# Second attention: four tiles instead of two split and stored before the stage, and all four read as it opens

## The reference, cut to what matters

```python
x = _layernorm(x + _L1_attn_ref(x, w_qkv, w_z, w_b, w_a, conv_w, dt_bias, a_log, norm_w, w_out))   # gated delta rule
x = _layernorm(x + _L1_xattn_ref(x, ctx_2048, ctx_2048, L1_xattn_gamma))                           # second attention
x = _layernorm(x + _L1_ffn_ref(x, gate_w, w_gate, w_up, w_down))                                   # experts, top 8 of 64

def _L1_xattn_ref(q, k, v, gamma):        # B=32, Dq=64, Lq=256
    qh = q.reshape(B, 8, 8, Lq)           # 8 heads of 8 rows each
    kh = k.reshape(B, 8, 8, Lk)
    vh = v.reshape(B, 8, 8, Lk)
    qk = jnp.einsum('bhdq,bhdl->bhql', qh, kh) / sqrt(8)
    sm = jax.nn.softmax(qk, axis=-1)
    return gamma * jnp.einsum('bhql,bhdl->bhdq', sm, vh).reshape(B, 64, Lq)
```

## Time and profile before

| | us |
|---|---|
| median of three runs | 3860.91 |
| the profiled execution | 3866.17 |
| its span, first to last instruction | 3864.1 |
| the second attention, barrier to its last scatters | about 2938 to 3320 |

### The profile page before, as it was taken

One profiled execution on the slowest core, in us unless ns is written; L12 is line 12 of the kernel. 1 busy time (PEld: TensorE's weight loads), 2 busy tenths in 40 slices (PEclk: granted clock), 3 DMA queues, 4 the chain that ended last, 5 costly groups with the idle time before them and its releaser, 6 DMA issues. The chain is left out here.

```text
span 3864.1 us, 101293 instructions
## 1 busy us (share of the span) xinstructions
PE 3395.9 (88%) x37544; PEld 2305.7 (60%) x37544; DVE 2397.3 (62%) x4366; ACT 1956.2 (51%) x5232; POOL 1966.2 (51%) x2830
## 2 busy tenths in 40 slices
PE   9998799886999999999999999999985878588876
PEld 6776466554666666666666666666663544344544
DVE  5554466344777777777777777777774766233433
ACT  1111255323666666666666666666652655243434
POOL 2232433243666556656555566655563455455654
PEclk9999799997999999999999999999996988699998
DMA  2000543001211111111111211111103543355545
GB/s 77 11 16 7 141 114 92 25 1 37 58 47 45 50 43 53 46 46 47 39 50 44 57 47 39 47 46 49 45 21 78 130 129 108 133 172 169 181 133 215
DMA packets 223140, 278.85 MB, mean 72 GB/s; under 512 B 58548, under 2 KB 186872, under 8 KB 216280
## 3 DMA queue, kind: packets, MB, share of 16 engines
q1 hardware_dynamic: 203340, 237.24, 21.5%
q0 software_dynamic: 18432, 34.96, 2.6%
q10 hardware_dynamic: 908, 0.27, 0.1%
HBM read 162.13 MB, written 125.83 MB: 75 GB/s over the span
## 5 line engine op out<-in xcount | busy, mean ns | idle before, releaser
L2153 PE MATMUL head_ring<-gd_xT,head_w 128*128 128x512 f32 x1024 | 522.7, 635 | 15.2 <-DMA head_w<-gd_w 10.4
L2607 POOL TENSOR_TENSOR head_V<-head_V,gd_ones 128x512 bf16<-128x512 f32 x128 | 133.0, 1040 | 476.1 <-DVE head_V L2451 476.1
L1504 POOL DMA_INDIRECT ytok<-exp_arena,exp_cur x256 | 250.6, 979 | 201.0 <-ACT exp_arena L1407 122.8
L2426 DVE SCALAR_TENSOR_TENSOR head_cb_V<-head_ring,head_taps,head_cb_V 128x504 f32<-128x504 f32 (+2 forms) x384 | 280.0, 729 | 12.9 <-ACT head_cb_V L2303 8.2
L2153 PEld LDWEIGHTS head_ring<-gd_xT,head_w 128*128 128x128 f32 x1024 | 182.8, 199 | 155.5 <-issue 132.5
L2272 PE MATMUL head_by<-head_wo,head_ogT 128*128 128x256 f32 x1024 | 258.2, 396 | 9.5 <-issue 6.1
L2162 PE MATMUL head_ring<-head_w,gd_xT 128*128 128x256 f32 x1024 | 256.0, 393 | 3.4 <-DVE head_cb_V L2426 3.0
L2457 DVE TENSOR_TENSOR head_Xs<-head_bx,head_join 128x512 bf16<-128x512 f32 x320 | 220.0, 687 | 60.5 <-PE head_bx L2194 54.0
L1076 DVE TENSOR_REDUCE cf_top<-cf_near 128x4 f32<-128x1024 f32 x128 | 155.0, 1219 | 115.5 <-PE cf_near L917 74.6
L1005 ACT ACTIVATE cf_prob<-cf_score 128x512 f32<-128x512 f32 x256 | 147.1, 604 | 138.4 <-PE cf_score L930 85.2
L2272 PEld LDWEIGHTS head_by<-head_wo,head_ogT 128*128 128x128 f32 x1024 | 186.8, 192 | 40.1 <-issue 14.5
(11 more groups left out here) (361 smaller groups left out, 9199.6 us busy)
## 6 DMA issues: line engine op xcount, KB each, us to landing
xbuf<-head_blank SPq DMA_DIRECT2D x64, 552.0 KB
exp_arena<-xbuf SPq DMA_DIRECT2D x64, 552.0 KB
head_gi<-scan SPq DMA_DIRECT2D x64, 256.0 KB
ytok<-head_blank SPq DMA_DIRECT2D x64, 256.0 KB
exp_arena<-ytok SPq DMA_DIRECT2D x14, 1024.0 KB, 12.7
moe_w<-moe_w SPq DMA_DIRECT2D x32, 384.0 KB
cb_Q<-qd SPq DMA_DIRECT2D x45, 192.0 KB
cb_K<-kd SPq DMA_DIRECT2D x45, 192.0 KB
```

Of the source, the lines that this page charges most:

```text
L1504: pool.indirect_dma_start(ytok, bass.IndirectOffsetOnAxis(ap=cur[i % AHEAD][s][:, b:b + 1], axis=0), y[i % RESULTS][s][:, b, :], None, bou ...
L2153: last = pe.matmul(b[:, :], w[:, c, FEAT[what]], xT[:, c, n % UNITS * N:n % UNITS * N + N], start=c == 0, stop=c == DC - 1)
L2426: dve.scalar_tensor_tensor(out=out, in0=by_seq(bank_of(f, n))[:, :, 0:SEQ - s], scalar=taps[:, TAP[f], KS - 1 - s:KS - s], in1=out, op0=AL ...
```

## The change

`Split.TILES` becomes 4. The scratch gets four places, indexed by `s = t % SLOTS` instead of `u = t % 2`. Tiles 2 and 3 are split in the last unit of the delta rule too, after its first correction (`uc1b` on ACT, ahead of `rr1` on POOL), into `ex`, which is dead by then, with the tapped V buffers `cb_V0`, `cb_V1` as rests. In `stage_cross` SP issues gathers 0 to 3 one behind the other without a wait; spread 2 and spread 3 are gone from that stage, with their casts and subtractions. ACT issues its eight DMAs first thing, once the first half of tile 0 has landed, and POOL fills the V buffers first thing.

```diff
 class Split:
-    TILES, PARTS, DH, WIDTH = 2, 3, 8, D
+    TILES, PARTS, DH, WIDTH = 4, 3, 8, D
...
 def gather(t):                      # stage_cross, SP: qd[u]/kd[u] -> qd[s]/kd[s]
...
                         u = t % 2
-                        if t == HELD + 1:
-                            gather(HELD)
-                        sp.wait_ge(gather_in[(t - 2) % SLOTS], START + (t - 2) // SLOTS * READS + READS)
-                        Split.spread(sp, part[u], qd, kd, u, cast_ready, (t - HELD) * PARTS, spread_in[u])
+                        s = t % SLOTS
+                        sp.wait_ge(gather_in[s], START + (t - SLOTS) // SLOTS * READS + READS)
+                        Split.spread(sp, part[u], qd, kd, s, cast_ready, (t - HELD) * PARTS, spread_in[u])
                     elif what == "gather":
-                        if t > HELD:
+                        if t >= HELD:
                             gather(t)
...
             def _(act):                     # stage_cross, ACT; the same lines are removed behind cast2 of tile HELD
+                act.wait_ge(ones_ready, START + 1)
+                act.wait_ge(first_in, START + READS)
+                for k in range(SLOTS):
+                    act.dma_start(K[k][NEAR:FULL, :, :], ones16[:, :]).then_inc(ones_in, 16)
+                act.dma_start(gate[:, :, :], A["moe_gateT"].rearrange("(c p) e -> p c e", p=P)).then_inc(route_in, 16)
+                for table, name in ((triangle, "triangle"), (queue, "queue_base"), (dest, "dest_base")):
+                    act.dma_start(table[:, :], A[name]).then_inc(route_in, 16)
...
                                 act.copy(U[:, b, :, :, :].rearrange("p h k e -> p (h k e)"), bu[b][:, :]).then_inc(u_ready, 1)
+                                if final and n == UNITS - 1 and what == "uc1b":
+                                    act.wait_ge(F_ready, at(turn, n))
+                                    for i in range(Split.PARTS):
+                                        cast(i, LATER)
...
                             if final and what == "rr1" and n:
                                 normed(n - 1)
+                                if n == UNITS - 1:
+                                    pool.wait_ge(silued["V0"], at(turn, n))
+                                    pool.wait_ge(silued["V1"], at(turn, n))
+                                    subtract(LATER)
...
-    qd = nc.dram_tensor("qd", [2, 24, ROWS * 2], BF16).ap()
-    kd = nc.dram_tensor("kd", [2, 40, ROWS * 2], BF16).ap()
+    qd = nc.dram_tensor("qd", [4, 24, ROWS * 2], BF16).ap()
+    kd = nc.dram_tensor("kd", [4, 40, ROWS * 2], BF16).ap()
```

More of the change, by code:

```diff
@@ L865, in gather @@
                         for i in range(PARTS):
-                            sp.dma_start(Q[s][i * length:i * length + length, heads, :].rearrange("p j c -> p (j c)"), qd[u, 0:length, held])\
+                            sp.dma_start(Q[s][i * length:i * length + length, heads, :].rearrange("p j c -> p (j c)"), qd[s, 0:length, held])\
                               .then_inc(landed, 16)
                             sp.dma_start(K[s][i * length:i * length + length, heads, :].rearrange("p j c -> p (j c)"),
-                                         kd[u, i * DH:i * DH + length, held]).then_inc(landed, 16)
+                                         kd[s, i * DH:i * DH + length, held]).then_inc(landed, 16)
                 for t, name in ((ident, "ident"), (gamma, "gamma")):
@@ L1016, in _ @@
                         act.copy(part[u][:, i, :, :], rest[u][:, :, :] if i else xc[:, n, :, :]).then_inc(cast_ready, 1)
[L1017 to L1023, removed]
                     elif what == "mid":
@@ L1159, in prefill @@
                     pool.memset(rows.row[:, :, Rows.BASE + 1:Rows.RANKS], 0.0).then_inc(rows_blank, 1)
+                prefill()
                 for what, n in timeline(POOL_PLAN):
@@ L1171, in _ @@
                             .then_inc(sub_ready, 1)
-                        if n == HELD and i == 1:
-                            prefill()
                     elif what == "tops":
@@ L1944, in stage_delta @@
             length = Split.PARTS * 2 * D
-            bits = [split_bits[:, t * length:t * length + length].rearrange("p (i h c) -> p i h c", i=Split.PARTS, h=2) for t in SPLIT]
-            left = [cb[f][:, :].rearrange("p (h c) -> p h c", h=2) for f in "KQ"]
-            cast_ready, sub_ready, spread_in = m.sems("cast_ready", 2), m.sems("sub_ready", 2), m.sem("spread_in")
+            more_bits = ex[:, :, :, :].rearrange("p h t i -> p (h t i)").bitcast(BF16)
+            bits = [(split_bits, more_bits)[t // 2][:, t % 2 * length:t % 2 * length + length].rearrange("p (i h c) -> p i h c", i=Split.PARTS, h=2)
+                    for t in SPLIT]
+            left = [cb[f][:, :].rearrange("p (h c) -> p h c", h=2) for f in CONV]
+            EARLIER, LATER = SPLIT[0:2], SPLIT[2:4]
+            cast_ready, sub_ready, spread_in = m.sems("cast_ready", len(SPLIT)), m.sems("sub_ready", len(SPLIT)), m.sem("spread_in")
             def unit_sem(name, per=1):
@@ L2281, in _, with cast @@
                 def _(act):
-                    def cast(i):
-                        for t in SPLIT:
+                    def cast(i, tiles):
+                        for t in tiles:
                             if i:
@@ L2343, in steps @@
                                     act.wait_ge(ex_ready, START + NK)
-                                    cast(0)
+                                    cast(0, EARLIER)
                                 elif final and n == UNITS - 1 and what == "ttc4":
-                                    cast(1)
+                                    cast(1, EARLIER)
                             elif what == "invc":
@@ L2354, in steps @@
                                 if final and n == UNITS - 1:
-                                    cast(2)
+                                    cast(2, EARLIER)
                             elif what in ("uc0a", "uc0b", "uc1a", "uc1b"):
@@ L2520, in normed, with subtract @@
                                   [rstd[:, t:t + 1] for t in each], n, TS)
+                    def subtract(tiles):
+                        for i in range(Split.PARTS - 1):
+                            for t in tiles:
+                                pool.wait_ge(cast_ready[t], START + i + 1)
+                                if i:
+                                    pool.wait_ge(sub_ready[t], START + i)
+                                pool.tensor_tensor(left[t], left[t] if i else xc[:, t, :, :], bits[t][:, i, :, :], ALU.subtract)\
+                                    .then_inc(sub_ready[t], 1)
                     def steps(turn, events, final=False):
@@ L2580, in steps @@
                                     pool.wait_ge(silued["Q"], at(turn, n))
[L2581 to L2587, removed]
+                                    subtract(EARLIER)
                             elif what == "less":
```

## The result

| | before | changed |
|---|---|---|
| median, same chip | 3860.33 us (12 runs) | 3869.78 us (12 runs) |
| ratio, 95% interval | | 1.0032 (1.0016 to 1.0048): slower |
| the profiled execution, its span | 3866.17, 3864.1 | 3876.25, 3874.1 |

The change costs 9.5 us by the medians and 12.4 us by the ratio, whose interval reaches from about 6 to 19 us; a later comparison on another chip gave 1.0038 (1.0026 to 1.0051), 12 to 14 us. The forecast was 4.

A forecast was written before the change was run, and what follows sets the result against it. The prediction took the first C product's start to decide: place 0 behind gather 3 in SP's queue put it at 2985.0 against 2981.0, +4.0 us, 0 for the rest, so 3860.91 + 4.0 = 3865 us; range 3857 to 3876.

The forecast's parts named there:

- the likeliest case: Opening of the second attention: first C product at 2985.0 instead of 2981.0, +4.0 us, range -1 to +7.7; chance 0.48.
- rival 2: POOL's wait before tile 4's subtractions: ACT's tables starve until the rows are through, +8.6 to +18.6 us; chance 0.26.
- One number decides: Second attention: the start of the first C product, 2981.03 before, shifts the end by as much as it shifts.
- The delta rule's tail at 0: Last unit of the delta rule: added casts, subtractions and writes cost 0, covered with 1.6 us to spare; bounds 0 and +5.9.
- Gather 1 left at 2967.7: SP's row reads in the opening: gather 1 lands at 2967.7 as before; bounds 2962.7 and 2970.
- R, the tables, at 2975: Time at which POOL has ACT's tables: 2975, the middle between 2972.5 and 2977.
- From R to C: From POOL having the tables to the first C product: 4.2 us to cf_topT done, then about 3.4 from place 0's issue.
- Gather 3 in front of place 0, 2985.0: SP's queue, second gate: gather 3 lands at 2984.7, place 0 0.3 us behind it, so first C product about 2985.0.
- Rival 1: Opening: ACT's queue keeps its share and place 0 gets past gather 3; -0.9, at best -4 us, 3857 to 3861; chance 0.17.
- the rule of the Trainium skill: DMA engines take turns between queues packet by packet, so ACT's small tables would not starve behind SP's rows; its result: 3857 to 3861.
- rival 3: Gain over 7.7 us: first C product before 2973.3, or mostly a clock rising earlier or falling less often later; chance 0.05.
- The clock and the rest of the stage: After the first C product: the clock's rise, about 8 us behind it, shifts with it; then the same 339 us.

The follow-up runs named there:

- the single edit: Changed kernel with POOL's wait for the four tables and its copy of cf_dest moved from the first tile to the third: 3853.32 us, ratio 1.0001.
- the last kernel: Kernel with late table wait, tables behind cf_topT, gather 3 in front; ones issued at once and place 0 issued by ACT on its queue: 3849.92 us, ratio 0.9999.

## Why the prediction was right or wrong

The range, 3857 to 3876, held the time, and slower had 0.29; the likeliest case, +4 us with its own range to +7.7, was too small, and the time came out as the milder case of rival 2, +8.6. The range held because it reached into rival 2, not because the sum was right. Point by point:

- **One number decides.** Right for the changed kernel: the first C product came 7.8 us later, and 14.9 us of it were worth 16.1 us between two kernels on one chip, 8.8 us 8.6 us on another. The two kernels with the ones at once don't fit it.
- **The delta rule's tail at 0.** Right, with 1.95 us of cover left where 1.6 were worked out. The writes had room too: SP still stood idle at the stage's end, 14.5 us instead of the 27.9 of the earlier trace rows.
- **Gather 1 left at 2967.7.** Wrong, and harmless: 19.5 us from the opening instead of 25.0, so 2962.2 on before's scale, at the lower bound (2962.7). The eight DMAs of ACT that start 2.4 us later are a likely reason: with the ones at once it landed at 26.4, with the wait for the first half of tile 0 at 18.3, and that is one edit. But the two were profiled on different chips, and in the changed kernel the writes of spread 2 have left too, so this is not shown.
- **R, the tables, at 2975: the step that failed.** Measured 39.15 us from the opening, so 2981.9 on before's scale; rival 2 had R = 2982 and C = 2989.6, and the measured C is 2988.9. I took the middle between 17.4 us from issue and 908 packets at 37 per us. But 37 per us was a rate beside gathers 0 and 1 alone, smaller rows among them; beside gathers 1 to 3 it was 24, the pace of the rows themselves (404 packets for 379). The 389 packets of the earlier trace rows that went as gather 1 thinned out were the row to go by.
- **From R to C.** Right: 4.1 us to `cf_topT` done (4.2), 2.9 more to the first C product (3.4). With the waits behind the copy in the order given, R's error passed on to C whole.
- **Gather 3 in front of place 0, 2985.0.** The gate is real and stood hidden behind R: with R gone it opens C at 38.5 to 40.0 from the opening, 2981.2 to 2982.7 on before's scale, where I had 2985.0. Its mechanism, the order of SP's queue, was wrong: place 0 in ACT's queue is as late. The 7.0 us per gather were too few as well: gathers 2 and 3 of the changed kernel took 18.7 us together behind gather 1, where I had 17.0; gather 3 was complete at 2980.9 on before's scale instead of 2984.7 only because gather 1 came sooner.
- **Rival 1 and the rule of the Trainium skill.** In 2963 to 2980 the two queues moved 404 packets for 379, which looks like turns. They did not keep the tables early: one small packet for one row is so slow that they ended with the rows. And in the 4 us shown above there were no turns. The Trainium skill ("DMA: Bandwidth & Descriptors", section Queues, rings and completion order) has each engine take turns by whole packets of typically 9 to 17 descriptors. The packets of this profile are single rows and pieces of rows, so one for one is finer than the page states, and a pause of 4 us is not ruled out by it; no run here shows where such a packet ends.
- **The chances.** Faster had 0.06, while rival 3, its only source, had 0.05; nothing hangs on it.
- **The clock and the rest of the stage.** The clock rose 7.6 us behind the first C product, as the prediction let it. The 339 us held PE work of 263 us instead of 273 at a clock of 0.86 instead of 0.83, chance of one execution.

## What to carry to other kernels

When row reads are issued earlier, look at what small transfers stand beside them, in every queue, and who waits for those: here the tables, place 0 and, unless put out at the opening, the ones ended when the rows ended. Put out what the first units need, and the rest of the reads behind the small transfer that opens the work (here gather 3 behind place 0, and waits for tables at the unit that uses them). A resource freed by a change helps only when the wait for it ended last; here two gates lay behind one another, and the single edit showed 6.2 of the 17 us.

## What the runs showed of the hardware

- Rows did not flow at one speed. From 2955 to 2978, with the ones at once, SP's queue was alone and moved 2.71 MB in 23 us, 0.118 MB per us at 77.0% busy; with the ones issued behind the first half of tile 0 it moved 1.75 MB in 12 us, 0.146 MB per us at 74.1%, with 69 packets of ACT's beside it. The kernel with four small DMAs put out 6.7 us earlier had slower reads, for over 20 us after these had landed. The two profiles are of different chips, and both kernels with the ones at once ran on the same one, so whether the edit or the chip did it stays open.
- Issuing can stall: ACT's last table, 8 KB, took 4.03 us to issue in the changed kernel and 0.45 before. It took 0.45 as well where the same eight DMAs came first but gathers 2 and 3 were held back, so the reads issued beside them matter; what was full is not shown.
- The trace names one wait where two end together: `cf_K<-cf_ones` was named where the ones and place 0 were complete within 0.9 us of each other, and with the ones early the same idle time stood there as "issue".
- A DMA completes in parts: 4 records for 24 KB on 3 rows, 13 for 24 rows, 16 for a table. In the last kernel 16 of the tables' 64 records came by 38.0 us from the opening and the next at 45.0, with rows moving between.
